# Attention layer on one core: where the score tiles that get a bias band stand, and when VectorE adds their bands

## The reference

```python
x = x + _layernorm(_L0_attn_ref(_layernorm(x, axis=-1), ...), axis=-1)
...
scores = jnp.einsum('bhqd,bhkd->bhqk', q, k)
position_bias = compute_bias(rel_bias, s, s)
scores = scores + position_bias
attn = jax.nn.softmax(scores.astype(jnp.float32), axis=-1).astype(scores.dtype)
out = jnp.einsum('bhqk,bhkd->bhqd', attn, v)
...
return out @ wo
```

## Time and profile before

| | before |
|---|---|
| median of 3 runs | 3097.6 us (3097.28 to 3097.96) |
| profiled execution, its own time | 3097.29 us |
| profiled execution, span of the instructions | 3095.5 us |
| TensorE busy | 2855.8 us (92%) |
| GpSimd busy | 2277.1 us (74%) |
| VectorE busy | 1891.3 us (61%) |
| ScalarE busy | 1651.8 us (53%) |
| mean granted TensorE clock | 0.975 of full speed |

### The profile page before, as it was taken

The page is one execution under the profiler, slowest core; times in us unless marked ns, Lnnn a source line. Parts: engine busy times, 40 slices in busy tenths (PEclk is TensorE's granted clock), DMA queues, the critical chain, the costliest instruction groups (busy, mean ns, idle before and its releaser), DMA issues. The chain is left out here.

```text
span 3095.5 us, 49866 instructions
## 1 busy us (share of the span) xinstructions
PE 2855.8 (92%) x18785; PEld 1055.8 (34%) x18785; DVE 1891.3 (61%) x4727; ACT 1651.8 (53%) x2139; POOL 2277.1 (74%) x1033
## 2 busy tenths in 40 slices
PE   3499999999999999999999999999999999988887
PEld 1133333333333333333333333333333333322343
DVE  5466656566566656566666556565656655576676
ACT  2255555555555555554555555555555455566566
POOL 0088878888888878887888888887888788887100
PEclk8699999999999999999999999999999999999999
DMA  7000000000000000000000000000000000100001
GB/s 156 22 1 1 1 1 18 2 1 2 18 1 2 1 1 18 2 1 1 18 1 1 2 18 1 2 1 1 18 1 1 1 8 1 56 1 1 28 1 55
DMA packets 45607, 36.53 MB, mean 12 GB/s; under 512 B 21510, under 2 KB 43782, under 8 KB 45366
## 3 DMA queue, kind: packets, MB, share of 16 engines
q1 hardware_dynamic: 45366, 33.34, 4.1%
HBM read 28.39 MB, written 11.34 MB: 13 GB/s over the span
## 5 line engine op out<-in xcount | busy, mean ns | idle before, releaser
L519 POOL TENSOR_TENSOR acc<-acc,prob 128x1024 f32<-128x1024 f32 x896 | 2117.2, 2363 | 444.4 <-ACT prob L888 368.6
L888 ACT ACTIVATE prob<-st 128x1024 f32<-128x1024 f32 x1024 | 1016.5, 1021 | 981.3 <-DVE st L1255 876.3
L609 PE MATMUL po<-prob,v 128*64 128x512 f32 x4096 | 995.3, 607 | 0.0
L579 PE MATMUL st<-qk 64*128 64x512 f16 x6144 | 843.6, 381 | 11.3 <-ACT prob L888 6.3
L1230 DVE CUSTOM_DVE_ANT_0 pre<-pre,ew 128x512 f32<-128x512 f32 x448 | 300.6, 713 | 569.0 <-issue 568.9
L1235 DVE CUSTOM_DVE_ANT_0 pre<-pre,tab 128x512 f32<-128x512 f32 x704 | 475.7, 715 | 108.6 <-issue 108.6
L579 PEld LDWEIGHTS st<-qk 64*128 64x128 f16 x6144 | 296.4, 95 | 340.1 <-ACT prob L888 46.2
L609 PEld LDWEIGHTS po<-prob,v 128*64 128x64 f32 x4096 | 248.9, 136 | 440.2 <-issue 365.4
L579 PE MATMUL st<-eq,ek 64*128 64x512 f16 x2048 | 393.0, 380 | 0.0
L591 PE MATMUL pre<-qk 64*128 64x512 f16 x1600 | 312.7, 387 | 81.1 <-DVE mpart L1235 31.6
L1238 DVE TENSOR_REDUCE mpart<-pre 128x2 f32<-128x1024 f32 x224 | 273.8, 1222 | 118.2 <-PE pre L591 116.2
(11 more groups left out here) (186 smaller groups left out, 2361.8 us busy)
## 6 DMA issues: line engine op xcount, KB each, us to landing
t_scratch<-w_scratch SPq DMA_DIRECT2D x2, 3072.0 KB
inv_r<-inv SPq DMA_DIRECT2D x260, 1.0 KB, 1.7
y<-x SPq DMA_DIRECT2D x2, 2048.0 KB, 11.3
qk<-x SPq DMA_DIRECT2D x8, 512.0 KB, 5.5
out<-qk SPq DMA_DIRECT2D x8, 512.0 KB, 3.6
w<-w_pairs SPq DMA_DIRECT2D x8, 384.0 KB, 3.9
t2f<-t_scratch SPq DMA_DIRECT2D x8, 384.0 KB, 4.6
t<-t_scratch SPq DMA_DIRECT2D x8, 384.0 KB, 3.3
```

The lines of the kernel that those rows point to most:

```text
L519: nc.gpsimd.tensor_tensor(acc[g % 2][:, :, :], a, prob[:, n % RING, :, :], ALU.add).then_inc(sum_p, 1)
L579: last = nc.tensor.matmul(st[:, 2 * (n % 2) + h, :], w[64 * h:64 * h + 64, :], t[64 * h:64 * h + 64, :], start=(r == 0), stop=(r == len(te ...
L609: last = nc.tensor.matmul(po[64 * h:64 * h + 64, :], v[:, g // CHUNKS, j, 64 * h:64 * h + 64], prob[:, n % RING, h, :], start=(s == 0), st ...
L888: nc.scalar.activation(prob[:, n % RING, :, :], st[:, 2 * (n % 2):2 * (n % 2) + 2, :], ACT.Exp).then_inc(exp_done, 1)
```

## The change

The near tiles move to other steps, so that all of them stand at odd steps (the second score tile of their pass): step 8 becomes 7, and 10 becomes 11. For chunks 0 and 3 too (3, 5, 7, 11, 13). And VectorE's program adds the band of the second score tile ahead of the pass's second maximum, where it was added behind it.

```diff
-BAND_STEPS = [3, 5, 8, 10, 13, 15]
+BAND_STEPS = [3, 5, 7, 11, 13, 15]
...
                     next_maximum(n)
                     if not last or n + 2 < STEPS:
                         bands = band(i, n + 2, bands)
-                    next_maximum(n + 1)
                     if not last or n + 3 < STEPS:
                         bands = band(i, n + 3, bands)
+                    next_maximum(n + 1)
                     rest(n)
                     rest(n + 1)
```

## The result

| | before | changed |
|---|---|---|
| median | 3097.68 us (14 runs, 3095.14 to 3099.74) | 3104.91 us (14 runs, 3103.14 to 3108.48) |
| profiled execution, its own time | 3097.29 us | 3108.27 us |
| profiled execution, span | 3095.5 us | 3106.5 us |

The ratio is 1.0025, 95% interval 1.0017 to 1.0033: slower by 7.2 us, a little over the 0.2% that the prediction took as the least that a measurement can tell. The direction was forecast (slower); the size was not: 22.4 us were forecast. The profiled execution of the changed kernel lies 3.4 us above its median, so its profile shows 11 us of difference and not 7.

A forecast was written before the change was run, and what follows sets the result against it. TensorE, busy 99% in the attention loop, was taken as the bound, so only its stops count. Terms summed to +2.9 us a pair, 20.4 for seven pairs plus 2.2 for the last: 22.6, so 3120 us, range 3102 to 3128.

The forecast's parts named there:

- the last head pair: Final head pair, with no pieces in its last two blocks and no projections in block 4: forecast 2.2 us slower.
- the band of step 13: In pass 10 this band (0.73 us) now runs ahead of the second maximum: forecast cost 0.17 us in block 5.
- The late band of step 11: Pass 8: band waits for the second score tile, moving everything behind it 0.53 us; block 5 passes 8 to 12 +0.31.
- Blocks 0 and 4, passes 4 to 6: Old stop of 0.61 us in pass 4 goes, new stop of 0.65 comes in pass 6: net +0.04 us.
- Blocks 1, 3, 5 and 7, passes 2 to 6: Early bands gain, step 7's band costs: blocks 1 and 5 net +0.06 us each, block 3 -0.69, block 7 +0.27.
- The tables: Block 6: early band delays tables and maximum; one L1202 still waits about 2 us for GpSimd, term +1.2 us a pair.
- The clock: Rival 4: the new stop in pass 10 drops TensorE's clock, 40 times 1.6 us, giving 3184 us; chance 0.04.
- rival 3: Block 6 tables all get through ahead of the GpSimd addition, saving 17 us in all: 3103 us; chance 0.07.
- Rival 2: Costs of the late band are half the forecast's and cancel the gains, no change: 3098 us; chance 0.06.

The follow-up runs named there:

- The experiment with the tables ahead of the band: Changed kernel with the band put back behind the second maximum in pass 10 of block 6 alone: 3083.55 us, ratio 0.9954 to the kernel before.
- the kernel with the steps alone: Kernel before with the new steps (3, 5, 7, 11, 13, 15) but the old order, band behind the second maximum: 3200.44 us, ratio 1.0340.

## Why the prediction was right and where it was wrong

The direction and the mechanism of the largest term were right. The size was off by three terms: a stop in block 4 that never came, the last head pair, and the band of step 13, which was put too high.

- **The late band of step 11.** Right in mechanism. The shift of 0.53 us was measured at every step of the chain, and so was the gain of 0.40 in pass 12. Passes 8 to 12 of block 5 cost +0.17 us (0.08 + 0.49 - 0.40) and not +0.31. The term that was mis-sized is the band of step 13 in pass 10: 0.17 was forecast for it, and from the second piece of pass 10 to the first of pass 12 it took 2.43 us for 2.39, so 0.04. The band took 0.69 us and not 0.73, and it began 0.08 us before line 1243 had ended, where I had it start behind it. Over all blocks but block 6, passes 8 to 12 were forecast at +1.94 us a head pair and measured +1.15, which is 5.5 us over seven head pairs.
- **Blocks 0 and 4, passes 4 to 6.** The step that failed in its mechanism. "Its exponential and all that ScalarE has behind it come 0.95 later", and so a new stop of 0.65 us, was worked out for both blocks from two lines of block 4. The stop needs line 894, and that is in block 0: there it came (6.22 us), in block 4 it did not. For these passes of block 4 +0.04 us was forecast and -0.62 measured, 4.6 us over seven head pairs. The sum itself had two slips. It took the old stop of 0.61 us out of the length of pass 4, but left it in the time of line 1216, 5.27 us; with step 7 back at 8, where that stop is gone, line 1216 starts at 4.64 us. And the band of step 7 moved it by 0.70 us, to 5.34, and not by 0.95. In block 0, where line 894 stands in between, line 1216 starts at 5.32 us with the stop and without it, so there the 0.95 us holds: 6.28. That block 0 came out right from the lines of block 4 is luck.
- **Blocks 1, 3, 5 and 7, passes 2 to 6.** Right: pass 6 of block 1 +0.35 for +0.32, short passes of 4.26 and 4.53 us for 4.28 and 4.53.
- **The tables.** The waits came as forecast (2.49 us for the first line 1202, none passed early), and pass 10 measured +1.1. With passes 8 and 12 block 6 came to +1.6 for a term of +1.2, that is 2.7 us more than forecast over seven head pairs. The reckoning behind the term was wrong: I let one wait stay as it was. The experiment with the tables ahead of the band shows that without the early band this pass would have been 1.0 us shorter than before; the early band took that and 1.1 us more.
- **The last head pair.** The other step that failed. Forecast +2.2 us; from its pass 0 to its last score tile it took 331.2 us for 333.2, so -2.0. Its blocks 5 and 6 carry layer norm work on VectorE and ScalarE, which I had not worked through: pass 10 of block 5 took 6.47 us for 7.08, passes 4 and 10 of block 6 took 9.24 for 10.47 and 6.19 for 7.71. Which of those instructions gained was not tried, so the cause stays open here.
- **The sum.** The span is 11.0 us longer in the profile, where 22.6 was forecast. Passes 8 to 12 (5.5), block 4 (4.6) and the last head pair (4.2), less block 6 (2.7), come to these 11.6 us; what is left beside them (the first head pair, the clock in block 6, the time before and behind the loop) nearly cancels. By stretches, 1.0 us came before the loop, 11.6 in seven head pairs, -2.0 in the last and 0.4 behind it. The other 3.8 us between the profiles and the medians are the spread of executions. In the profile of the changed kernel pass 12 of block 6 took 6.46 to 7.35 us and in that of before 6.05 to 7.43, by where the clock changed; whether this makes up the spread was not tried.
- **The rivals.** The clock did not fall for the stop of 1.16 us in pass 10: the granted clock stayed at 1.00 from 1410 to 1421 us, and pass 12 of blocks 1 to 5 is no slower than its own sum. The tables did not get through (rival 3); that the median, 3104.9, lies near this rival's 3103 is chance. Rival 2, a cancelling, was nearer to the truth than it was given: the loss is a third of the forecast.
- **A reading.** "The slices show 99%" is too much. The slices show a 9, which is 90% or more, and from 149 to 2527 us TensorE was busy 97% of the time. Nothing in the sum hangs on it.

## What to carry to other kernels

When a step moves to another slot of a pipeline, work out first when its input is ready there. An order that looks free of waits can start a chain later, and the price stands where the chain meets the busiest engine again, here one pass on. Do the sum for every block that has its own side work, and look each side instruction up in each block, before one block's rows are made to stand for another. And when a stop is found, move the head of the chain behind it, not the instruction next to the stop: one line put ahead of a maximum was worth 39 us here, more than the 24 of the new order by itself.

## What the runs showed of the hardware

How long VectorE's table instructions take depends on what GpSimd has ready. The same copy of 128 x 768 took 0.56 us at its shortest, ahead of the loop, and 1.00, 1.48, 1.64 or 2.11 in block 6 of four of these kernels, and a line 1204 of 128 x 64 took 0.24 or 2.39. With the band behind the tables, and one GpSimd addition less under them, a pass was 2.1 us shorter. The Trainium skill (SBUF — State Buffer, on the shared port pair) describes this as a lock that one instruction holds to its end; the waits here agree with it: in all twelve kernels every long one of these instructions in block 6 ended 0.05 to 0.42 us behind the end of a GpSimd addition. So an input that is ready sooner for GpSimd can lengthen VectorE's stretch, though neither engine has more work.

TensorE's clock after a long stop: a stop of 4.72 us in block 6 of the changed kernel was followed by a piece of 0.61 us for 0.39, which is the level of 1.2 GHz, and by a granted clock of 0.61 from 1464 to 1471 us. After the shorter stop of 2.62 us in the changed kernel with the tables ahead the next piece took 0.61 us too, and the mean granted clock over the next pass was 0.77; after the stop of 1.16 us it was 1.00. The view by windows, first the changed kernel (busy time of TensorE, its weight loads, VectorE, ScalarE and GpSimd, then the granted clock):

```profile
1464.00:1471.00 7.00, 6.85 (x32) 2.53 (x34) 2.48 (x9) 3.07 (x3) 3.25 (x2) 0.61 0.00 0
```

and the changed kernel with the tables ahead:

```profile
1452.60:1458.80 6.20, 6.16 (x34) 2.21 (x34) 2.90 (x8) 4.00 (x5) 4.35 (x2) 0.77 0.00 0
```

The length of the stop alone does not decide it. The stop of 2.6 us was followed by the lower clock in six head pairs of seven (0.79 over pass 12, which took 6.05 to 6.07 us) and by full speed in the first (5.65 us). In the kernel with the steps alone a longer stop, 3.0 us, was followed by full speed in five of seven (5.65 us again). What else decides it was not tried.
